# Layer 0's first tensor product in wide operations, with ScalarE weighting in PSUM

## What is computed

```
msg_s = (s_n @ Ws_src)[src] + (s_n @ Ws_dst)[dst]         # 64 scalars
msg_v = (v_n . Wv_src)[src] + (v_n . Wv_dst)[dst]         # 32 vectors of 3
y0, y1 = rsh[:, 0], rsh[:, 1:4]
w1 = rbf @ W_rbf                                          # 224 weights per edge
m1_s = [w_ss * msg_s * y0,  w_vv0 * dot(msg_v, y1)]       # first tensor product
m1_v = [w_sv * msg_s * y1,  w_vs * msg_v * y0,  w_vv1 * cross(msg_v, y1)]
a = alpha_dot . leaky(m1_s @ W_alpha)                     # 4 heads
val_s, val_v = m1_s @ Ws_val, m1_v . Wv_val
val_v = val_v * sigmoid(val_s @ Wg);  val_s = sigmoid(val_s)
m2_s, m2_v = the same product of val_s, val_v with y0, y1 # second tensor product
h = [m2_s @ Ws_vlin, m2_v . Wv_vlin]                      # 4 heads of 40 values
out = sum over dst of softmax(a) * h, projected, added to the node
```

## Time and profile before

| what | value |
| --- | --- |
| device time, median of 3 runs | 12166.53 us (12155.68 to 12169.12) |
| the profiled execution | 12098.74 us, of which the span of the trace is 12096.9 us |
| PE busy | 9397.7 us, 78% of the span |
| DVE busy | 9136.3 us, 76% |
| ACT busy | 7003.3 us, 58% |
| POOL busy | 6367.4 us, 53% |

### The profile page before, as it was taken

How to read it: one execution, slowest core, us unless ns; L and a number is a source line. 1 busy time by engine, 2 the same in 40 slices (tenths; PEclk the granted TensorE clock), 3 DMA queues, 4 the chain that set the end, 5 groups by cost and what they waited for, 6 DMA issues and landing times. The chain is left out here.

```text
span 12096.9 us, 245491 instructions
## 1 busy us (share of the span) xinstructions
PE 9397.7 (78%) x46500; PEld 6592.8 (55%) x46501; DVE 9136.3 (76%) x32454; ACT 7003.3 (58%) x26255; POOL 6367.4 (53%) x9502
## 2 busy tenths in 40 slices
PE   4421188888888888888888788887788888788887
PEld 1211177777777777777777344445433335444445
DVE  6702078888888888888887899995565555899996
ACT  0000067777777777777776555553566666676764
POOL 0677646666666666666542455551355553455551
PEclk9855589999999999999998999996799999999997
DMA  6433211111111111111111343333222223343333
GB/s 262 53 66 70 64 31 31 30 30 30 30 31 30 31 30 30 31 30 31 27 17 38 82 87 86 87 85 46 43 53 52 52 52 54 84 87 85 86 85 60
DMA packets 1798441, 691.91 MB, mean 57 GB/s; under 512 B 1586190, under 2 KB 1677258, under 8 KB 1798346
## 3 DMA queue, kind: packets, MB, share of 16 engines
q0 software_dynamic: 219136, 411.56, 14.6%
q1 hardware_dynamic: 1572154, 275.26, 13.5%
q10 hardware_dynamic: 7056, 4.02, 0.1%
HBM read 514.24 MB, written 171.77 MB: 57 GB/s over the span
## 5 line engine op out<-in xcount | busy, mean ns | idle before, releaser
L963 POOL DMA_INDIRECT shared<-table,rec x2640 | 2560.4, 970 | 2508.8 <-issue 1058.4
L1045 PE MATMUL bank<-tp,oh 128*128 128x480 f32 (+1 forms) x5280 | 2407.3, 552 | 6.3 <-DVE tp L1122 4.6
L997 ACT ACTIVATE tp<-tp,rec 128x64 f32<-128x64 f32 x7920 | 2030.3, 335 | 234.1 <-DVE tp L1093 153.2
L1037 PE MATMUL bank<-w_fc,hT 128*128 128x448 f32 x2640 | 1368.5, 601 | 701.5 <-ACT hT L981 447.9
L1680 ACT ACTIVATE shared<-bank 128x512 f32<-128x512 f32 x1760 | 973.6, 595 | 961.9 <-PE bank L1755 955.1
L1045 PEld LDWEIGHTS bank<-tp,oh 128*128 128x128 f32 x5280 | 921.0, 195 | 856.8 <-issue 843.5
L1755 PE MATMUL bank<-ident,tp 128*128 128x128 f32 x7040 | 1054.0, 299 | 265.5 <-ACT tp L813 218.2
L1093 DVE TENSOR_TENSOR tp<-bank,shared 128x256 f32<-128x256 f32 x1320 | 560.2, 424 | 924.3 <-PE bank L1045 613.4
L782 POOL DMA_INDIRECT rec_dst<-ACC x784 | 813.5, 1038 | 602.5 <-issue 571.9
L1755 PEld LDWEIGHTS bank<-ident,tp 128*128 128x128 f32 x7040 | 889.9, 154 | 303.3 <-ACT tp L813 253.6
L1644 POOL DMA_INDIRECT gat<-table,rec x880 | 866.7, 985 | 277.0 <-issue 190.7
(11 more groups left out here) (248 smaller groups left out, 22541.0 us busy)
## 6 DMA issues: line engine op xcount, KB each, us to landing
shared<-table,rec POOLq DMA_INDIRECT x2640
rec_dst<-tp SPq DMA_DIRECT2D x44, 900.0 KB, 23.6
ACC<-in_attrs SPq DMA_DIRECT2D x56, 623.0 KB
rec_src<-tp SPq DMA_DIRECT2D x44, 730.0 KB, 19.9
efr<-rec_src SPq DMA_DIRECT2D x440, 64.0 KB
efr<-rec_dst SPq DMA_DIRECT2D x440, 64.0 KB
ACC<-in_attrs SPq DMA_DIRECT2D x196, 130.0 KB
rec<-rec_dst SPq DMA_DIRECT2D x1320, 10.0 KB
```

Source lines behind the costliest of these rows:

```text
L963: nc.gpsimd.indirect_dma_start(out=gatx[:, u, g, 0:L.row], out_offset=None, in_=tables[L.n][:, :], in_offset=IOff(ap=rec[:, u, g, L.idx:L. ...
L997: done = nc.scalar.activation(t[:, g, lo:lo + 64], t[:, g, 0:64], ACT.Copy, scale=rec[:, u, g, L.y + k:L.y + k + 1])
L1037: nc.tensor.matmul(pW[u % 2][:, 0:448], hT[:, u % 2, :], fc2[:, :], start=True, stop=True)\
L1045: done = nc.tensor.matmul(pS[u % 2][:, 0:TW], oh[:, u, g, :], tp[:, u % 2, g, 64:64 + TW], start=g == 0, stop=g == G - 1)
```

## The change

In layer 0's edge loop:

- The message is written to a row `rows` in ACC, 160 columns wide, and by a second operation its first 64 vector columns once more behind it, so that the vector's three axes can be read in cyclic order.
- The columns of the weights are put in the order of the other loops. ScalarE multiplies the 96 columns of w_ss and w_vs by y0, in place in PSUM: two new operations a step, in the step in which the weights are made, behind the six of the second product.
- `product_vector` and `product_pool` go. VectorE's first product is one operation of 256 elements for both weighted scalars (in front of the distances), and behind the distances two of 288, one of 192, a reduction of 192 to 64, and one each of 192, 64 and 192. POOL has no part of it any more, and gathers at the step's start.
- ScalarE's six operations of the first product stand in front of its copies of the turned edge features and one-hots, no longer behind them.
- The two gate operations become one; the two weighing operations and the copy become one of 328 elements. For this the bank `pH` has 41 columns per head, and the 41st is set to 1 once.
- The running maximum is written back behind the weighing, no longer between the maximum and the one-hot. The register with e's block number is that of d's a step before, in three steps of four.
- The second product keeps its operations and its part on POOL, with the last two VectorE operations exchanged.

```
-                nc.vector.tensor_tensor(t_sv[:, :, :], w[:, :, 64:128], s, ALU.mult).then_inc(sv_ready.h, 1)
...
+                        nc.vector.tensor_tensor(rows[:, u % 2, :, 0:F], gat[:, u % 4], pBv, ALU.add)
+                        nc.vector.tensor_tensor(rows[:, u % 2, :, F:F + 64], gat[:, u % 4, :, 64:128],
+                                                pBv[:, :, 64:128], ALU.add).then_inc(msg_ready.h, 1)
...
+                        nc.vector.tensor_tensor(tp[:, 0, :, 0:128].rearrange("p g (j c) -> p g j c", j=2),
+                                                w[:, :, 0:128].rearrange("p g (j c) -> p g j c", j=2),
+                                                rows[:, u % 2, :, 0:64].unsqueeze(2).to_broadcast([P, G, 2, 64]),
+                                                ALU.mult).then_inc(sv1_ready.h, 1)
...
+                        for g in range(G):
+                            done = nc.vector.tensor_tensor(
+                                vy0[:, g], ranges(row[:, g, 64:65], [[32, 3], [32, 3], [1, 32]]),
+                                ranges(rec[:, u % 4, g, L.y:L.y + 1], [[2, 3], [1, 3], [0, 32]]), ALU.mult)
+                        done.then_inc(vy_ready.h, 1)
+                        nc.vector.tensor_tensor(tv[:, :, :, 64:96], v, along(128), ALU.mult)
+                        ve.wait_ge(vy_ready.h, vy_ready.done(i, u))
+                        nc.vector.reduce_sum(t_sum[:, :, :], vy0[:, :, 0].rearrange("p g k c -> p g c k"), AX.X)\
+                            .then_inc(joined.h, 1)
+                        nc.vector.tensor_tensor(cross0[:, :, :, :], vy0[:, :, 1], vy0[:, :, 2], ALU.subtract)\
+                            .then_inc(crossed.h, 1)
+                        ve.wait_ge(joined.h, joined.done(i, u))
+                        nc.vector.tensor_tensor(t[:, :, 128:160], t_sum[:, :, :], w[:, :, 160:192], ALU.mult)
+                        ve.wait_ge(crossed.h, crossed.done(i, u))
+                        nc.vector.tensor_tensor(tv[:, :, :, 96:128], cross0[:, :, :, :], along(192), ALU.mult)\
+                            .then_inc(tp1_ready.h, 1)
...
+                        if a:
+                            ac.wait_ge(w_ready.h, w_ready.done(*a))
+                            for g in range(G):
+                                y0w = pW[:, 224 * g + 64:224 * g + 160]
+                                last = nc.scalar.activation(y0w, y0w, ACT.Copy, scale=rec[:, a[1] % 4, g, 2:3])
+                            last.then_inc(w_scaled.h, 1)
...
-                        nc.vector.tensor_copy(mrow, mnew[:, u % 2, :])
+
+                    def held(i, u, block):
+                        nc.vector.tensor_copy(flat(M[:, block, :]), mnew[:, u % 2, :])
...
-                            block_e = block_of(ve, *e)
+                            block_e = last_block[0] if last_block else block_of(ve, *e)
+                        last_block[:] = [block_d] if d and d[1] % 4 else []
```

198 lines of the change are left out of this document (89 added, 109 removed).

## The result

| what | before | after |
| --- | --- | --- |
| device time, median of 4 runs each | 12161.1 us | 12707.02 us (12703.63 to 12729.5) |
| ratio to before, 95% interval | 1 | 1.0454 [1.0436, 1.0472] |
| span of the profiled execution | 12096.9 us | 12727.8 us |
| mean granted clock of TensorE | 0.897 | 0.849 |

The forecast was 11955 us with a range of 11850 to 12100. The change costs 546 us instead of saving 211, and only 6% had been given to a slower result.

What follows compares the result with a forecast made beforehand. VectorE was taken to set layer 0's step, 10.89 us when plain. A gain of 0.60 us a step, 264 us in 440, less 53 us for TensorE's half clock, left 211 us: 12166.5 to 11955 us, range 11850 to 12100.

Steps and rivals of the forecast that it cites:

- the paragraph on ScalarE and POOL: ScalarE's two added operations and new order, POOL's lost multiplications and earlier gathers: priced at zero, up to 0.3 us a step.
- the slower rival: TensorE at half clock 40% of the time, its work in more pieces: 11.78 us a step, 12421 us; chance 0.06.
- the signs that the prediction had named: Trace signs for or against it; wrong if, among others, the step stays near 11 with VectorE idle ahead of the maximum.
- difference to one-hot: VectorE, running maximum's copy moved out from between the two: 0.47 to 0.11 us, gain 0.36 us a step.
- the first product, with its weighted scalars: VectorE from t_sv to the logits, fewer operations: 2.56 to 2.35 us, gain 0.21 us a step.
- maximum to logits: VectorE's stretch holding the difference, one-hot and first product: 4.87 us before, 4.3 us expected in the trace after.
- copy back: Running maximum's copy, now behind VectorE's weighing: 0.11 us a step lost.
- plain step: Layer 0 step without the loop's branch, message to message: 10.89 us before, about 10.25 us expected.
- The head of the step: Second message operation, 0.20 us: free in plain steps beside one saved register read, 0.05 us a step lost over four.
- The clock stays up: Rival: denser TensorE falls to half clock less often; gain 0.72 us a step, 317 us, 11850 us; chance 0.14.
- the 0.17: Layer 0 loop before: us a step lost to TensorE's half clock, beyond what its spare time hides.
- VectorE held by the gathers: Rival: two-SBUF-input VectorE operations beside POOL's gathers lose 0.45 us a step, 198 us; 12153 us, no change; chance 0.05.

Runs made afterwards that it cites:

- e14: Changed kernel with one unused POOL multiplication of 96 elements between the scatters and the gathers; 11717.3 us, ratio 0.9633 to the kernel before.
- e1: Changed kernel, but POOL's gather for the next pair waits for the message of the present one; 11693.23 us, ratio 0.967 to the kernel before.
- e13: Changed kernel with two unused POOL multiplications of 96 elements between the scatters and the gathers; 11750.1 us, ratio 0.9647 to the kernel before.
- e5: Kernel before with its old products, but POOL's scatter and next gather put together, four indirect DMAs in a row; 13143.61 us, ratio 1.0769.
- e2: Changed kernel with the next pair's gather issued in front of the scatter, row of four kept; 12531.97 us, ratio 1.0349 to the kernel before.
- e8: Changed kernel with each gathered row 32 elements in place of 160, same count of rows and DMAs; 12734.0 us in one run.
- e7: Changed kernel with layer 0's scatters as plain DMAs to fixed places, gathers still indirect; 11829.91 us in one run, later layers on other data.
- e4: Changed kernel with each gather a plain DMA of 128 neighbouring rows, scatters still indirect; 11630.97 us in one run.
- e6: Changed kernel with only the second of a step's two gathers waiting for the message; 12468.79 us, ratio 1.021 to the kernel before.

## Why the prediction was wrong, step by step

**The step that failed** is in the paragraph on ScalarE and POOL: "POOL loses five multiplications and does its gathers at once; it is not waited for", priced at zero. Every word of it is true of the profile before. POOL was the engine with time to spare, and nobody waits for it now either: in the stretch of 1000 us it is GpSimd that waits, 470 us for `vsv` alone.

```profile
POOL t_cr L1599 <- DVE vsv L1884: 470.3, 77, 7.0
```

What was missed is what "at once" meant. These are GpSimd's rows from scatter to gather before:

```profile
3529.71 1.13 POOL L1631 DMA_INDIRECT rec_src<-ACC  x1 [0.31 <-issue]
3531.49 0.54 POOL L801 TENSOR_TENSOR t_cr<-msg,rec 128x64 f32<-128x64 f32 x2 [0.65 <-DVE msg L1848]
...
3533.04 1.01 POOL L1644 DMA_INDIRECT gat<-table,rec  x1 [0.15 <-issue]
```

The multiplications (1.4 us) with their wait for the message (0.65 us) had kept four indirect DMAs apart: two, 2.2 us of something else, two. To remove them was to move the gathers, and they came against the scatters. The prediction looked at what the five multiplications cost, not at what they separated. e14 puts an operation of 0.38 us in their place, which opens a gap of 1.23 us, and the 0.98 us of the steps without scatter are there in the others too.

Hence also the sentence against the slower rival, "nothing in the change adds a wait to TensorE", was wrong: the row of four added them. The rival's supposed share of half clock (0.40) is near the measured 0.38, but not its mechanism, more pieces of TensorE's own work; that the shares agree is luck. The waits of up to 3.5 us come on top, so that the step is 12.81 us and not 11.78. Of the signs that the prediction had named, one appeared: VectorE idle ahead of the maximum, though in a step of 12.81 us and not near 11.

**The VectorE arithmetic was right**, which e1 shows, where the rest is out of the way (rows of e1 above against the earlier trace rows):

| term | forecast, us a step | e1 |
| --- | --- | --- |
| difference to one-hot | 0.47 to 0.11 | 0.08 (3503.47 to 3503.55) |
| the first product, with its weighted scalars | 2.56 to 2.35 | 2.33 (0.38 + 1.95) |
| maximum to logits | 4.87 to 4.3 | 4.04 (3502.32 to 3506.36) |
| gates | 0.33 to 0.27 | 0.26 (3507.21 to 3507.47) |
| weighing | 0.54 to 0.41 | 0.41 (3508.07 to 3508.48) |
| copy back | 0.11 lost | 0.09 |
| plain step | 10.25 | 9.94 (median of all) |
| step with the branch | 11.05 | 10.85 (3501.41 to 3512.26) |

What the forecast missed here lay mostly in two places. `dlt` to the next operation had been 0.24 us and is 0.08 (before, the weighted scalars stood behind it; now they stand ahead of it); and the second product got 0.07 shorter (1.77 us from L1850 at 3508.57 to L1896 at 3510.34, for 1.84) with the exchange that was priced at zero. The head of the step was nearly right: spread logits to maximum 1.96 us (3500.36 to 3502.32) for 1.88 before (3540.25 to 3542.13), so the second message operation and the saved register read nearly cancel.

**TensorE** waits 0.63 us ahead of the logits in e1 and not at all ahead of the first product, as forecast (0.7 and nearly nothing). The clock there is 0.97. So the half-clock share fell from 0.13 to 0.07, where the forecast had more of the half clock show and gave back 0.12 us a step for it. What half clock costs hardly moved: the mean step lies 0.21 us over one at full clock before (11.27 for 11.06) and 0.18 in e1 (10.31 for 10.13). *The clock stays up*, held at 0.14, was the truer of the two in that nothing is given back, once the row of four is gone; but most of the 0.17 that it hoped to win was not won. Together e1's step is 0.97 us shorter than before's, 427 us in 440 steps (its ratio gives about 400 us), against 211 forecast. The forecast for the arithmetic was too careful by a factor of about two; the sign was lost on a queue that it had priced at zero.

**VectorE held by the gathers** is refuted. In e1 the two operations of 288 elements (3504.41) run beside a gather (3504.21 to 3505.17) and last 0.82 us, as in layer 1's loop. Beside POOL's multiplications they do lose time: in the kernel after, L1852 lasts 0.43 us beside one and 0.28 us beside a scatter, the 0.15 us of the earlier trace rows. By the Trainium skill (page "SBUF — State Buffer", section "SBUF: two separate sides") a VectorE operation with two SBUF inputs and a GpSimd operation that reads SBUF exclude each other, and the one that starts later waits; the trace shows a loss of that kind beside GpSimd's multiplications, and none beside its indirect DMAs.

```profile
3501.45 0.75 POOL L1604 TENSOR_TENSOR t_dot<-vsv,rec 128x96 f32<-128x96 f32 x2
3501.92 0.43 DVE L1852 TENSOR_TENSOR tp<-rec,vsv 128x128 f32<-128x128 f32 x1
...
3514.80 1.03 POOL L1572 DMA_INDIRECT rec_src<-ACC  x1 [0.16 <-issue]
3515.26 0.28 DVE L1852 TENSOR_TENSOR tp<-rec,vsv 128x128 f32<-128x128 f32 x1
```

## What to carry to other kernels

Before work is taken from an engine that nobody waits for, write down that engine's new order and look at which DMAs now stand next to each other: what an idle engine does between two transfers may be all that keeps them apart. Four indirect DMAs of GpSimd at 0.3 us from each other cost this loop a fifth of its time, two pairs with 0.8 us or more between them cost 0.1 us a step at most (e1, e13, e14, with scatter and without). And when every engine's busy share falls at once while the time rises, look for signals that come later than the record they belong to: the waiting instruction's start against the end of what released it.

## What the runs showed of the hardware

- A row of four DMA_INDIRECT of GpSimd at 0.30 us goes with completion signals of TensorE that come 0.9 to 1.3 us late on the average and up to 3.2 us, while the next matmuls start behind each other in time. Steps: 10.3 us for two and two, 12.8 for four (e1, after); in the old kernel 11.3 and 13.7 (before, e5). Late are the signals that fall due from about the third's start to half a microsecond behind the fourth's end, 98% of them, and those due well before or after come in time (after, and e2 with the pairs exchanged). Late signals a step: 3.7 after, 3.8 in e5, 3.7 in e8; 0.85 in e1, 0.9 in e7, 0.09 in e14, 0.01 in e4. Three and then a gap do little beside that (e6). Signals of VectorE and ScalarE are not held (after).
- Plain DMAs in place of either pair don't do it (e4, e7), a fifth of the gathers' bytes does (e8). How the two meet in the chip no run shows. The Trainium skill (page "Perfetto Trace Analysis", section "DMA Instruction — SWDGE (GPSIMD)") says that the end of such a record on GpSimd is that of making the descriptors, not of moving the data. The trace agrees: in the kernel after, the last packet of GpSimd's queue ends 1.3 us behind the fourth record (median).
- The signals that were held back in one step often come in a burst, 60 ns apart. With the matmuls behind them starting in time, this speaks for the delivery being held and not the array; it doesn't prove it, since the ends of matmuls are modelled.
- The clock amplifies it. TensorE's share at 1.2 GHz goes 0.07 with two and two, 0.33 in e6's mixture, 0.38 with four. In the excerpt after, TensorE stands 1.90 us ahead of L1738 at 3508.83, and the next eight turns take 1.95 us, after 1.04 for the eight before the wait.
- The version for use is e1 or e14, at 0.967 [0.965, 0.9689] and 0.9633 [0.9598, 0.9668] of the kernel before; their intervals overlap, and the step with scatter is 10.31 and 10.24 us. e1 needs no operation without use, e14 has fewer late signals.
